# Post-LN transformer block in fp32 on one core: gelu's four high parts rounded on ScalarE instead of VectorE

## The reference

```python
def _L0_attn_ref(x, wq, wk, wv, wo):
    ...
    q = fractional_rope(q, ROTARY_BASE)
    k = fractional_rope(k, ROTARY_BASE)
    inv_sqrt_dh = DH ** (-0.5)
    q = q * inv_sqrt_dh
    k = k * inv_sqrt_dh
    s = jnp.einsum('bhik,bhjk->bhij', q, k)
    ...
    s = s - 1e+30 * mask
    p = jax.nn.softmax(s, axis=-1)
    o = jnp.einsum('bhij,bhjv->bihv', p, v)
    ...
def _L0_ffn_ref(x, w1, b1, w2, b2):
    ...
    bw1 = _binarize(w1)
    h = jnp.einsum('bsd,hd->bsh', x, bw1) + b1
    h = jax.nn.gelu(h, approximate=False)
    bw2 = _binarize(w2)
    out = jnp.einsum('bsh,dh->bsd', h, bw2) + b2
    return out
x = L0_attn_x
x = _layernorm(x + _L0_attn_ref(x, L0_attn_wq, L0_attn_wk, L0_attn_wv, L0_attn_wo), axis=-1)
x = _layernorm(x + _L0_ffn_ref(x, L0_ffn_w1, L0_ffn_b1, L0_ffn_w2, L0_ffn_b2), axis=-1)
```

## Time and profile before

| | |
|---|---|
| time, median of 3 executions | 344.56 us (342.98 to 345.43) |
| profiled execution: its time | 340.74 us |
| profiled execution: its span | 338.9 us |
| PE busy | 300.7 us, 89% |
| DVE busy | 268.0 us, 79% |
| ACT busy | 200.2 us, 59% |
| POOL busy | 139.8 us, 41% |
| granted TensorE clock, mean | 0.985 of full |

### The profile page before, as it was taken

The page is one execution under the profiler, slowest core; times in us unless marked ns, Lnnn a source line. Parts: engine busy times, 40 slices in busy tenths (PEclk is TensorE's granted clock), DMA queues, the critical chain, the costliest instruction groups (busy, mean ns, idle before and its releaser), DMA issues.

```text
span 338.9 us, 5451 instructions
## 1 busy us (share of the span) xinstructions
PE 300.7 (89%) x1739; PEld 234.6 (69%) x1739; DVE 268.0 (79%) x637; ACT 200.2 (59%) x362; POOL 139.8 (41%) x183
## 2 busy tenths in 40 slices
PE   3689799999999999998999999999999999885760
PEld 3567657875888677975888677966898587643540
DVE  2777637788578869888887968987888968889995
ACT  2256535795468745795378637793479556821533
POOL 1300301348033763158324753358324743095342
PEclk9999999999999999999999999999999999999896
DMA  7502001200040004200140005000210004000204
GB/s 234 168 2 62 1 3 57 66 2 0 5 121 3 1 0 127 61 2 1 51 137 0 0 0 166 20 0 0 84 40 0 2 0 126 1 0 0 64 0 125
DMA packets 26451, 14.67 MB, mean 43 GB/s; under 512 B 832, under 2 KB 25920, under 8 KB 26432
## 3 DMA queue, kind: packets, MB, share of 16 engines
q1 hardware_dynamic: 26432, 14.42, 14.2%
HBM read 10.23 MB, written 4.19 MB: 43 GB/s over the span
## 4 chain that ended last, share of the span: by engine, by line
PE 55%; DVE 16%; ACT 13%; issue 8%; POOL 3%; DMA 2%; DVEq 0%; POOLq 0%; ACTq 0%
PE wide L413 13%; PE acc L454 8%; PE turn L440 6%; PE acc L462 4%; DVE hid_hi L1098 4%; ACT hid L822 3%; PE acc L512 3%; PE acc L511 3%; PE wide L499 3%; PE wide L501 2%; PE wide L500 2%; DVE qkT_lo L1089 2%; ACT L822 2%; PE turn L471 2%; ACT qkT_hi L816 2%
## 5 line engine op out<-in xcount | busy, mean ns | idle before, releaser
L806 ACT ACTIVATE prob<-wide,negmax 128x128 f32<-128x128 f32 (+3 forms) x64 | 47.3, 743 | 51.2 <-DVE negmax L1084 50.9
L308 POOL TENSOR_TENSOR hid_lo<-hid,hid_hi 128x1024 fp32r<-128x1024 f32 x26 | 61.6, 2371 | 27.1 <-DVE hid_hi L1098 27.1
L1084 DVE TENSOR_REDUCE negmax<-wide 128x1 f32<-128x128 f32 (+3 forms) x64 | 47.2, 750 | 28.7 <-PE wide L416 28.4
L454 PE MATMUL acc<-probT,xa 128*128 128x512 f32 (+3 forms) x176 | 66.7, 495 | 0.1
L300 POOL TENSOR_TENSOR qk_tok<-rot_cos,rot_sin 128x512 f32<-128x512 f32 x16 | 20.7, 1291 | 80.5 <-DVE rot_sin L1111 80.5
L413 PE MATMUL wide<-qkT_hi 128*128 128x512 f32 (+2 forms) x96 | 43.3, 451 | 6.2 <-ACT prob L806 6.0
L812 ACT ACTIVATE probT<-turn 128x512 f32<-128x512 f32 (+1 forms) x64 | 31.3, 515 | 24.3 <-PE turn L440 23.4
L440 PE MATMUL turn<-ident,prob 128*128 128x128 f32 x288 | 42.3, 274 | 1.8 <-DVE x1T_lo L1089 0.8
L1098 DVE CAST hid_hi<-hid 128x1024 fp32r<-128x1024 f32 x27 | 37.6, 1400 | 1.4 <-ACT hid L822 1.4
L454 PEld LDWEIGHTS acc<-probT,xa 128*128 128x128 f32 x176 | 29.8, 192 | 12.0 <-issue 10.5
L440 PEld LDWEIGHTS turn<-ident,prob 128*128 128x128 f32 x288 | 32.9, 141 | 7.2 <-issue 3.4
(11 more groups left out here) (140 smaller groups left out, 674.7 us busy)
## 6 DMA issues: line engine op xcount, KB each, us to landing
xq<-in_L_attn_x_dram SPq DMA_DIRECT2D x8, 512.0 KB, 3.8
xa<-in_L_attn_x_dram SPq DMA_DIRECT2D x8, 512.0 KB, 3.7
out_dram<-y_out SPq DMA_DIRECT2D x6, 512.0 KB, 3.0
cos_sb<-in_cos_dram SPq DMA_DIRECT2D x1, 512.0 KB, 4.4
sin_sb<-in_sin_dram SPq DMA_DIRECT2D x1, 512.0 KB, 6.2
w_sb<-in_L_ffn_w_dram SPq DMA_DIRECT2D x2, 256.0 KB, 5.2
out_dram<-y_out SPq DMA_DIRECT2D x2, 256.0 KB, 2.5
out_dram<-x SPq DMA_DIRECT2D x2, 256.0 KB, 3.0
```

Source lines behind the costliest of these rows:

```text
L308: pool.tensor_tensor(hid_lo[:, j, :], hid[:, j, :], hid_hi[:, j, :].bitcast(F32), ALU.subtract).then_inc(s_hid_lo, 1)
L454: ins = pe.matmul(acc[g][:, lo:BANK], xa[:, j, :], probT[g][:, j, lo:BANK], start=j == 0, stop=j == KEYS[g] - 1)
L806: act.activation(prob[:, ROW[r]:ROW[r + 1]], wide[r % 2][:, 0:(r + 1) * P], ACT.Exp, bias=negmax[:, r:r + 1], accum_out=rowsum[:, r:r + 1] ...
L1084: dve.tensor_reduce(negmax[:, r:r + 1], wide[r % 2][:, 0:(r + 1) * P], axis=AX.X, op=ALU.max, negate=True).then_inc(s_max, 1)
```

## The change

ScalarE makes the four high parts. In a step it does hidden_high(0) behind the first pair of qkT_high, hidden_high(1) behind the second pair, and hidden_high(2) behind gelu(3); hidden_high(3) follows in the next step, behind the exponentials of rows 0 and 1, and in the last step at its end. VectorE's list loses them. GpSimd's low part of block 3 moves from the end of the step to the next one, behind the factors of the second norm. The roundings of the last sequence, in halves (L1332), stay on VectorE.

```diff
@@ gpsimd, step
-                q, f, z = (b, 1), (b, -1), (b, -3)
+                q, f, o, z = (b, 1), (b, -1), (b, -2), (b, -3)
...
-                def hidden_low(j):
+                def hidden_low(j, c):
 
-                    if last and j % 2 == 1:
+                    if last and j % 2 == 1 and c == f:
                         return
-                    pool.wait_ge(s_hid_hi, at(NF, f, j + 1))
+                    pool.wait_ge(s_hid_hi, at(NF, c, j + 1))
...
                 if has_z:
                     second_factors(z)
+                if has_o:
+                    hidden_low(3, o)
                 if has_f:
                     first_factors()
...
                 if has_f:
-                    hidden_low(0)
-                    hidden_low(1)
-                    hidden_low(2)
-                    hidden_low(3)
+                    hidden_low(0, f)
+                    hidden_low(1, f)
+                    hidden_low(2, f)
...
@@ scalar, step
+                def hidden_high(j, c):
+                    act.wait_ge(s_gelu, at(NF, c, j + 1))
+                    act.activation(hid_hi[:, j, :], hid[:, j, :], ACT.Copy).then_inc(s_hid_hi, 1)
...
                     exponentials(1)
+                if has_o:
+                    hidden_high(3, o)
+                if has_a:
                     exponentials(2)
...
                     qkT_high(1)
                 if has_f:
+                    hidden_high(0, f)
                     gelu(2)
                 if has_q:
                     qkT_high(2)
                     qkT_high(3)
                 if has_f:
+                    hidden_high(1, f)
                     gelu(3)
+                    hidden_high(2, f)
+                if last:
+                    hidden_high(3, f)
...
@@ vector
-                def hidden_high(j, c):
-                    dve.wait_ge(s_gelu, at(NF, c, j + 1))
-                    dve.tensor_copy(hid_hi[:, j, :], hid[:, j, :]).then_inc(s_hid_hi, 1)
...
             def hidden_prev():
 
-                dve.wait_ge(s_gelu, at(NF, end1, NF))
-                dve.tensor_copy(hid_hi[:, NF - 1, :], hid[:, NF - 1, :]).then_inc(s_hid_hi, 1)
                 hidden_low(NF - 1, NF)
```

More of the change, by code:

```diff
@@ L1247, in step @@
                     row_max(1)
-                if has_o:
-                    hidden_high(3, o)
                 if has_z:
@@ L1298, in step @@
                     statistics2(1, end2)
-                if has_f:
-                    hidden_high(0, f)
                 if has_q:
@@ L1303, in step @@
                     qkT_low(1)
-                if has_f:
-                    hidden_high(1, f)
-                if has_q:
                     qkT_low(2)
-                if has_f:
-                    hidden_high(2, f)
-                if has_q:
                     qkT_low(3)
```

## The result

The changed kernel takes 346.05 us, the median of 20 runs (343.75 to 348.31), the kernel before on the same chips 342.71 us, 20 runs (339.63 to 345.43). The ratio is 1.0103, with a 95% interval of 1.0074 to 1.0132: about 3.5 us slower. In the profiled executions the span went from 338.94 to 343.18 us, +4.24.

What follows compares the result with a forecast made beforehand. The prediction took TensorE to be the main bound, losing time at seams (ScalarE's last three gelus, next step's first scores). Five seams at 0.9 plus 0.75, less 1.1 in the drain, gave +4.2 us: 348.8, range 344.8 to 352.2.

Steps and rivals of the forecast that it cites:

- The cost of a copy: On ScalarE: a rounding copy of 1024 columns takes 1.02 us, 0.90 from start to start.
- The reserve: TensorE's spare time from scores(1) to scores(4)'s second matmul, 0.84 to 1.18 us a seam; the most the change can gain there.
- The fourth low part decides: On GpSimd, low part 3 behind the second norm's factors makes the loss 0.9 us, not 0.4, in each of five seams.
- second_norm(0) hidden: On VectorE, normalizations beside the moved low part end about 127.3, before scores(5) ends at about 128: 0.7 us to spare.
- The drain: Behind the last step: one rounding less (0.6) and an earlier first copy (0.45), together 1.1 us less; ends 0 and 2.5.
- the far end: Behind the last step: 2.5 us less, if the three roundings before 298.81 also held up GpSimd's factors.
- only the clock: Rival written for experiment 1: the shorter drain only reflects where it started, as with TensorE's clock; within 0.5 us of before.
- The sum: Whole kernel: 5 x 0.9 + 0.75 - 1.1 = +4.2 us, 348.8 against the median 344.56.
- The dearer copy: Rival, on ScalarE: copies take 1.20 and 1.09 us like gelu, +2.2 on the sum, 351.0 us; chance 0.20.
- The cheap copy: Rival, on ScalarE: copies take 0.60 and 0.48 us, seams cost almost nothing, 342 to 343.5 us; chance 0.05.
- TensorE and GpSimd meet better: Rival, in the seams: low part 3 costs nothing, a seam costs 0.45, 345 to 346.5 us; chance 0.23.
- The clock: Rival, in the seams: TensorE's wait before scores(1) drops its clock to 1.2 GHz, +18 us, 366; chance 0.02.

Runs made afterwards that it cites:

- experiment 6: Kernel before, with the last step's roundings and every sequence's third (behind gelu(3)) and fourth (behind exp(1)) on ScalarE: 333.91 us against 343.12, ratio 0.9716.
- experiment 2: Changed kernel, with GpSimd's low part of block 3 again ahead of the second norm's factors: 343.99 us, ratio 1.0061 against the kernel before.
- experiment 3: Kernel before, roundings on VectorE, with only GpSimd's low part of block 3 moved behind the second norm's factors: 350.34 us, ratio 1.0252.
- experiment 1: Kernel before, with only the last step's four roundings moved to ScalarE: 339.15 us against 341.96, ratio 0.9929.
- experiment 4: Kernel before, with only the fourth rounding of each sequence moved to ScalarE, behind exp(1): 337.40 us, ratio 0.9900.

## Why the prediction was right

**The cost of a copy.** Predicted 1.02 us and 0.90 from start to start; measured 1.05 to 1.10 (mean 1.078) and 0.95. The step took the slope of the rows; the Trainium skill's estimate of 1.04 and 0.95 for it ("ScalarE: Activation LUTs", What ACT_TABLE_LOAD costs) was nearer: the trace agrees with its spacing, and its length is 0.04 short of the mean. gelu(3) ended at T + 5.19 for 5.05, and copy 1 at T + 4.09 for 3.97.

**The reserve.** Right. It was read as what TensorE took between scores(1) and scores(4) beyond what it needs, and said to be all that the relief on VectorE could bring. The loss at scores(4) came out within 0.05 us in every seam, and experiment 6 turned the same reserve into a gain of the same size. That closeness is partly luck: scores(1) came 1.71 to 1.78 us late, not 1.6, and TensorE then took 6.17 us to the second matmul of scores(4), not 6.25. The exponential was also a nearer thing than forecast. Exponential 0 was to end 0.9 us before TensorE could start scores(2) (119.5 for 120.4, which is T + 7.6 for T + 8.5). It ended at T + 7.81, and TensorE started at T + 7.99: in this trace the third score block begins 0.6 us before the end of the products ahead of it, which the step had not counted.

**The fourth low part decides.** Its cost was right, and is shown from two sides: taking its place back lets TensorE's fourth block come 0.5 us sooner per seam (experiment 2), and moving it alone costs 8.6 us (experiment 3). In the changed kernel the same move costs only 2.6, for two reasons of like size: the factors and the low part end 0.6 us sooner than in experiment 3 (T + 14.48 for 15.08), and TensorE, held up by gelu(3), wants the low part 0.5 later (T + 14.1 for 13.6). That it "decides more" than the copies in front of gelu(3) did not come out: of the 6.1 us of the seams 2.6 are the low part's and 3.5 the copies'. The loss in all was 1.04 to 1.10 per seam, predicted 0.9. From copy 1 on, GpSimd's queue runs about 0.1 us behind the forecast to the end of low part 3 (T + 14.48 for 14.39), which is the dearer copies, and TensorE starts 0.15 behind that end where I had 0.1.

**second_norm(0) hidden.** Right. On VectorE the four normalizations that lie beside the moved low part end at 127.89, and the row maximum behind them still has to wait for TensorE:

```profile
125.72 2.17 DVE L1159 TENSOR_SCALAR y_out<-res,ln 128x128 f32<-128x128 f32 x4
129.05 0.96 DVE L1097 TENSOR_REDUCE negmax<-wide 128x1 f32<-128x768 f32 x1 [1.16 <-PE wide L417]
```

**The drain: the term that was mis-sized.** Predicted -1.1 with ends of 0 and 2.5; measured -2.8, and 3.1 less in experiment 1 alone. Of the 2.8, 1.9 stand ahead of residual1 and 0.9 behind it.

The 1.9 are the edit's. The step counted the rounding of 0.68 and the earlier first copy, but left the roundings before them out, although it named them as the far end: "if the three roundings before 298.81 also held up GpSimd's factors". They did. Beside VectorE's three roundings, GpSimd's small operations of the factors took three times as long as in the changed kernel. Before, then after:

```profile
296.98 1.91 DVE L1098 CAST hid_hi<-hid 128x1024 fp32r<-128x1024 f32 x3
...
297.68 0.66 POOL L263 TENSOR_TENSOR ln<-stat 128x8 f32<-128x8 f32 x1
298.30 0.65 POOL L264 TENSOR_TENSOR ln<-stat 128x8 f32<-128x8 f32 x1
```

```profile
304.56 0.21 POOL L263 TENSOR_TENSOR ln<-stat 128x8 f32<-128x8 f32 x1
```

The power started 1.76 us sooner. It was also 0.98 shorter: before, a low part of VectorE (1.23 us from 301.70) ran beside its start, in the changed kernel that part starts at 308.42, 0.3 before the power ends.

The 0.9 behind residual1 go with TensorE's granted clock, and that they come from the edit is not shown. Some 9 us behind residual1 ScalarE's last gelus wait for a burst of products on TensorE (L755 and L756, one line further down in the changed kernel). It starts at 318.61 in the kernel before, at 323.74 in the changed one, at 315.78 in experiment 4. The first 1.2 us of it in the three traces, by stretches (PE, PEld, DVE, ACT and POOL busy, then the clock):

```profile
318.60:319.80 1.20, 1.20 (x4) 0.91 (x5) 1.17 (x3) 0.02 (x1) 0.65 (x1) 0.53 0.00 0
```

```profile
323.70:324.90 1.20, 1.17 (x7) 1.06 (x8) 1.17 (x3) 0.42 (x1) 0.69 (x1) 1.00 0.00 0
```

```profile
315.80:317.00 1.20, 1.20 (x8) 1.02 (x9) 1.17 (x3) 0.49 (x1) 0.63 (x1) 1.00 0.00 0
```

Before, the clock falls to 1.2 GHz as the burst begins, and ScalarE does next to nothing in this stretch; in the other two it is full in the whole stretch and falls behind it. From residual1 to the end they take 29.35, 28.46 and 28.11 us. TensorE had waited less for the low part in the changed kernel (0.9 us at most, not 2.8), but in experiment 4 it waited 2.8 as before, with residual1 at its old place. So the shorter wait is not needed for the later fall, and part of the -2.8 may be the chance of one execution. The rival that I wrote down for experiment 1 (only the clock) is wrong for the 1.9 and open for the rest.

**The sum.** +4.2 was right in size because two terms erred against each other, and that is luck. The seams were off by 1.9 (7.1 for 5.25: 0.5 is a late transfer, 0.9 the larger loss per seam, 0.4 the longer matmul behind the wait), the drain by 1.7 the other way (0.8 ahead of residual1, 0.9 with the clock). The measured +3.5 us lies on the 1% line.

**The rivals.** The dearer copy (1.20 and 1.09) fell with the measured 1.08 and 0.95. The cheap copy fell too. That TensorE and GpSimd meet better did not happen: GpSimd had no gap from low part 1 to low part 3, as forecast. Of that rival the drain's far end (2.5) came nearer the truth than the 1.1 in the sum. The clock stayed full through the seams.

## What to carry to other kernels

Ask of every moved operation on which side of the one that the bounding engine waits for it lands: four equal copies of 1.05 us went to ScalarE, and the two behind gelu(3) were worth 0.8 to 1.2 us a seam together while each of the two in front of it cost about 0.8. A move that looks like bookkeeping (one low part behind one normalization's factors) can cost nearly as much as the change that it comes with, so price it apart, and in the place where it will stand: alone it cost 8.6 us, in the changed kernel 2.6. And measure how long the bounding engine really needs between its two waits: that difference is the whole gain to be had, and here it gave the loss of the change and the gain of a better version at that place within 0.05 us. Then look whether a gain lives on: in experiment 4 two seams lost 0.35 us again 7 us later, to a wait for another engine.

## What the runs showed of the hardware

A rounding on VectorE does not run beside a low part on GpSimd: it ends when the low part is over. The seam into step 3 in the kernel before, VectorE's four roundings and then GpSimd's first three low parts:

```profile
109.95 0.69 DVE L1098 CAST hid_hi<-hid 128x1024 fp32r<-128x1024 f32 x1 [0.22 <-ACT hid L822]
...
112.74 0.94 DVE L1098 CAST hid_hi<-hid 128x1024 fp32r<-128x1024 f32 x1
...
114.31 2.36 DVE L1098 CAST hid_hi<-hid 128x1024 fp32r<-128x1024 f32 x1
...
117.72 1.92 DVE L1098 CAST hid_hi<-hid 128x1024 fp32r<-128x1024 f32 x1
```

```profile
110.72 2.41 POOL L308 TENSOR_TENSOR hid_lo<-hid,hid_hi 128x1024 fp32r<-128x1024 f32 x1 [2.63 <-DVE hid_hi L1098]
113.76 2.36 POOL L308 TENSOR_TENSOR hid_lo<-hid,hid_hi 128x1024 fp32r<-128x1024 f32 x1 [0.63 <-DVE hid_hi L1098]
116.75 2.35 POOL L308 TENSOR_TENSOR hid_lo<-hid,hid_hi 128x1024 fp32r<-128x1024 f32 x1 [0.63 <-DVE hid_hi L1098]
```

The first rounding has no low part beside it and takes 0.69. The other three end at 113.68, 116.67 and 119.64, each 0.54 or 0.55 us behind the end of a low part (113.13, 116.12, 119.10), however early they started; and each low part waits 0.63 us for its rounding. So the two engines took turns, one low part every 3.0 us. With the roundings on ScalarE, which took 1.05 to 1.10 beside the same low parts, GpSimd starts the second and the third 2.32 us apart (the first two 3.0, with gelu(3) between their copies). The third and the fourth rounding (2.36 and 1.92 us here) are the ones whose removal experiments 4 and 6 show to pay, which fits; that their length is the reason was not tested apart. I had read these rows for their sum alone. It works the other way round too, as the drain's rows show: GpSimd's 0.21 us operations took 0.65 beside roundings.

In each of the eight traces other than that of the kernel before, exactly one transfer of xa (512 KB) landed late, 4.8 to 5.9 us behind its issue where the others of the steps took 3.4 to 3.9. A matmul waited up to 1.15 us for it, and the next gelu(0) came up to 1.4 late. In the changed kernel it was issued at 131.15 and landed 5.15 later:

```profile
136.34 0.70 PE L455 MATMUL acc<-probT,xa 128*128 128x512 f32 x1 [0.25 <-DMA xa<-in_L_attn_x_dram]
```

It was always one issued between 128 and 168 us, in step 3 or 4, whatever the edit. The medians' difference of experiment 6 (9.2 us) agrees with the seams and the drain (9.1) when it is left out, and not as well when it is counted (7.8), so the kernel before may well meet it in other executions; with one trace of that kernel this is not shown.
